# Gate and up of an FFN by Strassen's method: seven block products for eight in 11 of 14 steps

## The reference

```python
def linear(x, w, su, sv):
    return jnp.einsum('bsh,oh->bso', x, w * (su @ sv))
def ffn(x):
    a = linear(x, gate_w, gate_su, gate_sv)     # 1792 x 512
    b = linear(x, up_w, up_su, up_sv)
    return linear(silu(a) * b, down_w, down_su, down_sv)
x = x + 0.5 * ffn(layernorm(x))
x = x + attention(layernorm(x))
x = x + 0.5 * ffn(layernorm(x))
```

## Time and profile before

| what | value |
|---|---|
| median of 3 runs | 1300.13 us (1299.88 to 1300.18) |
| the profiled execution | 1300.31 us, its span in the profile 1299.0 us |
| PE, DVE, ACT, POOL busy | 1270.3, 719.8, 668.6, 403.8 us |
| chain that ended last, PE's share | 95% |

### The profile page before, as it was taken

How to read it: one execution, slowest core, us unless ns; L and a number is a source line. 1 busy time by engine, 2 the same in 40 slices (tenths; PEclk the granted TensorE clock), 3 DMA queues, 4 the chain that set the end, 5 groups by cost and what they waited for, 6 DMA issues and landing times.

```text
span 1299.0 us, 18149 instructions
## 1 busy us (share of the span) xinstructions
PE 1270.3 (98%) x6694; PEld 1084.5 (83%) x6694; DVE 719.8 (55%) x1896; ACT 668.6 (51%) x1623; POOL 403.8 (31%) x331
## 2 busy tenths in 40 slices
PE   5999999999999999999999999999999989999999
PEld 4788888888888888888888888888888878888887
DVE  7443444676566566566566566566566754333333
ACT  3222222247667667667667666666666762222221
POOL 4233222725314315315315315315314321222220
PEclk9999999999999999999999999999999999999999
DMA  7022222101001101001001001001001010111111
GB/s 268 34 101 101 100 86 100 65 2 49 33 1 49 34 1 50 33 1 49 34 1 50 33 1 49 33 1 50 33 1 49 1 49 1 49 49 49 49 49 65
DMA packets 15015, 60.18 MB, mean 46 GB/s; under 512 B 2064, under 2 KB 2736, under 8 KB 12880
## 3 DMA queue, kind: packets, MB, share of 16 engines
q1 hardware_dynamic: 14544, 58.47, 12.4%
q10 hardware_dynamic: 384, 0.56, 0.1%
HBM read 45.91 MB, written 13.11 MB: 45 GB/s over the span
## 4 chain that ended last, share of the span: by engine, by line
PE 95%; DVE 2%; ACT 2%; issue 1%; POOL 0%; DMA 0%; SPq 0%; DVEq 0%; ACTq 0%
PE bank L187 29%; PE bank L188 28%; PE bank L189 28%; PE bank L333 5%; PE bank L312 2%; PE bank L216 1%; PE bank L315 1%; ACT prob L528 0%; ACT prob L537 0%; PE bank L204 0%; POOL w_l_early L879 0%; DMA x_rows<-x 0%; DVE probT_l L798 0%; DVE stats L634 0%; PE bank L199 0%
## 5 line engine op out<-in xcount | busy, mean ns | idle before, releaser
L528 ACT ACTIVATE prob<-prob,neg_top 128x128 f32<-128x128 f32 (+3 forms) x256 | 140.9, 552 | 75.8 <-DVE neg_top L787 75.2
L922 POOL TENSOR_TENSOR rows<-rows,row_root_y 128x640 f32<-128x640 f32 x64 | 80.7, 1261 | 272.2 <-DVE row_root_y L630 272.2
L543 ACT CAST probT_h<-bank 128x512 fp32r<-128x512 f32 x160 | 84.6, 596 | 136.9 <-PE bank L333 136.9
L879 POOL TENSOR_TENSOR w_l_late<-raw_late,w_h_late 128x512 fp32r<-128x512 f32 (+1 forms) x64 | 93.8, 1488 | 178.2 <-ACT w_h_late L425 178.2
L680 DVE TENSOR_TENSOR d<-bank,silu 128x512 f32<-128x512 f32 x56 | 38.7, 691 | 197.3 <-PE bank L189 193.1
L916 POOL TENSOR_TENSOR square<-rows 128x640 f32<-128x640 f32 x64 | 80.3, 1255 | 205.5 <-ACT rows L507 205.5
L537 ACT ACTIVATE prob<-prob,inverse 128x128 f32<-128x128 f32 (+3 forms) x256 | 123.0, 554 | 1.8 <-DVE inverse L792 1.8
L440 ACT CAST d_hi<-d 128x512 fp32r<-128x512 f32 x56 | 34.8, 621 | 168.2 <-DVE d L680 168.2
L187 PE MATMUL bank<-w_h_late,xnT_hi 128*128 128x512 f32 (+1 forms) x352 | 121.2, 344 | 0.0
L189 PE MATMUL bank<-w_h_late,xnT_lo 128*128 128x512 f32 (+1 forms) x352 | 118.6, 337 | 0.0
L188 PE MATMUL bank<-w_l_late,xnT_hi 128*128 128x512 f32 (+1 forms) x352 | 118.3, 336 | 0.0
(11 more groups left out here) (121 smaller groups left out, 3390.5 us busy)
## 6 DMA issues: line engine op xcount, KB each, us to landing
raw_late<-w_qkv SPq DMA_DIRECT2D x8, 1536.0 KB, 6.3
raw_early<-ffn_w SPq DMA_DIRECT2D x21, 512.0 KB, 4.8
scaled<-raw_early SPq DMA_DIRECT2D x21, 512.0 KB, 2.6
raw_late<-scaled SPq DMA_DIRECT2D x21, 512.0 KB, 4.8
raw_late<-w_o SPq DMA_DIRECT2D x8, 1024.0 KB, 4.8
y<-x_rows SPq DMA_DIRECT2D x8, 256.0 KB, 2.0
x_rows<-x SPq DMA_DIRECT2D x6, 256.0 KB, 5.6
x_rows<-x ACTq DMA_DIRECT2D x2, 256.0 KB, 4.4
```

Source lines behind the costliest of these rows:

```text
L528: last = act.activation(p, p, ACT.Exp, bias=neg_top[:, h:h + 1], scale=-1.0, accum_out=total[:, h:h + 1])
L543: act.copy(probT_h[:, j, :, :], banks[r.bank][:, :].rearrange("p (h q) -> p h q", h=G)).then_inc(probT_hi_done, 1)
L879: return pool.tensor_tensor(lo, raw, hi.bitcast(F32), ALU.subtract)
L922: pool.tensor_tensor(row, row, by, ALU.mult).then_inc(rows_normed, 1)
```

## The change

In the steps 1 to 5 of pass 0 and 1 to 6 of pass 1 gate and up are seen as a product of 2 x 2 blocks. The weights' blocks are a11, a12 (chunk 0, features 0 to 255 and 256 to 511) and a21, a22 (chunk 1), the tokens' blocks b11, b21 (batch 0, the two halves of the features) and b12, b22 (batch 1). Eight block products of 12 matmuls become seven, by Strassen's method in Winograd's form: four sums of weight blocks s1 to s4 (`mix_weights`, on GpSimd, each step), four sums of token blocks t1 to t4 (`mix_tokens`, on VectorE, once a pass, from whole tokens that GpSimd and ScalarE put together first), and additions of the products. Products 1, 6, 7 and 4 are added up in the two banks Y (0 and 1) one behind the other; after each of the first three ScalarE copies the partial sum out (`partial_sum`) before the next product may be added. Products 5 and 3 use the two banks Z (2 and 3) in the same way, `down`, the scale products and product 2 the four others. VectorE adds the copies to the banks of products 2, 5 and 3 (`add_up`) and multiplies gate and up from SBUF. All work of `down` and of the scale products stays. `gated(0,0)` of a step comes from products 2 and 1, (c=1, b=1) from 5 and 7, (1,0) from 4, and (0,1) from 3 and 6; the last of them is finished in the next step. The sum blocks get rounded part and rest like all weights.

The core of the diff (PE, then ACT, DVE, POOL):

```diff
+SEVEN = {1: ("a11", "b11", "y"), 2: ("a12", "b21", "x"), 6: ("s2", "t2", "y"), 5: ("s1", "t1", "z"),
+         7: ("s3", "t3", "y"), 4: ("a22", "t4", "y"), 3: ("s4", "b22", "z")}
+Y_BANKS, Z_BANKS = range(0, 2), range(2, 4)
+PLAIN = (0, STEPS - 1), (0,)
+A = ("a11", "a12", "a21", "a22")
...
+            def product(p, s, m):
+                block, tokens, sum_in = SEVEN[m]
+                _, w_h, w_l = place(p, block)
+                pe.wait_ge(ffn_lo, split_nth(p, s, block) + 1)
+                if tokens in MIXES:
+                    at = MIXES.index(tokens)
+                    pe.wait_ge(mix_lo_done, p * len(MIXES) + at + 1)
+                    t_h, t_l = (t[:, at, :, :] for t in mixes[p])
+                else:
+                    k, b = 2 * (int(tokens[1]) - 1), int(tokens[2]) - 1
+                    t_h, t_l = (t[:, k:k + 2, b * S:(b + 1) * S] for t in (xnT_hi, xnT_lo))
+                for half in range(2):
+                    bank = {"x": None, "y": Y_BANKS[half], "z": Z_BANKS[half]}[sum_in]
+                    r, bank = result("product", p, s, m, half, bank=bank)
+                    for k in range(2):
+                        w = slice((2 * k + half) * P, (2 * k + half + 1) * P)
+                        last = matmul3(bank[:, :], (w_h[:, w], w_l[:, w]), (t_h[:, k, :], t_l[:, k, :]),
+                                       k == 0 and m in (1, 2, 5), k == 1, True)
+                    last.then_inc(full[r.bank], 1)
...
+            def ffn_second(p):
+                product(p, 1, 1)
+                product(p, 1, 2)
+                down(p, 0, 1)
+                if p == 0:
+                    scale_weights(1, "down")
+                product(p, 1, 5)
+                product(p, 1, 6)
+                product(p, 1, 7)
+                if p == 0:
+                    scale_weights(2, "gu0")
+                product(p, 1, 4)
+                if p == 0:
+                    scale_weights(2, "gu1")
+                product(p, 1, 3)
             def ffn_step(p, s):
+                product(p, s, 1)
+                down(p, s - 1, 0)
+                if p == 0:
+                    scale_weights(s + 1, "gu0")
+                product(p, s, 2)
+                product(p, s, 6)
+                if p == 0:
+                    scale_weights(s + 1, "gu1")
+                down(p, s - 1, 1)
+                if p == 0:
+                    scale_weights(s, "down")
+                product(p, s, 5)
+                product(p, s, 7)
+                product(p, s, 4)
+                product(p, s, 3)
+            def ffn_last(p):
+                if p == 0:
+                    rotation[0] = range(BANKS)
+                    down(p, STEPS - 2, 0)
+                    gate_up(p, STEPS - 1, 0, 0, (1,))
+                    down(p, STEPS - 2, 1)
+                    scale_weights(STEPS - 1, "down")
+                    gate_up(p, STEPS - 1, 1, 0)
+                    gate_up(p, STEPS - 1, 0, 1, (0,))
+                    down(p, STEPS - 1, 0)
+                else:
+                    down(p, STEPS - 1, 0)
+                    down(p, STEPS - 1, 1)
...
+            def partial_sum(p, s, m, half):
+                r = results["product", p, s, m, half]
+                act.wait_ge(full[r.bank], r.nth)
+                act.copy(more[p][3][:, (1, 6, 7).index(m), half, :], banks[r.bank][:, :]).then_inc(evac[r.bank], 1)
...
+            def mix_hi(p, *ats):
+                for at in ats:
+                    act.wait_ge(mix_done, p * len(MIXES) + MIX_ORDER.index(at) + 1)
+                    act.copy(mixes[p][0][:, at, :, :], mixed_tokens(at)).then_inc(mix_hi_done, 1)
...
+            def ffn_second(p):
+                partial_sum(p, 1, 1, 0)
+                partial_sum(p, 1, 1, 1)
+                split(p, 1, "a22", "s2")
+                silu_of(p, 1, 0, 0)
+                product_hi(p, 1, 0, 0)
+                split(p, 1, "s1")
+                mix_hi(p, 2, 3)
+                split(p, 1, "s3", "s4", "d0", "d1")
+                if p == 0:
+                    stack_factors(2, "gu0")
+                    stack_factors(2, "gu1")
+                partial_sum(p, 1, 6, 0)
+                partial_sum(p, 1, 6, 1)
+                partial_sum(p, 1, 7, 0)
+                silu_of(p, 1, 1, 1)
+                partial_sum(p, 1, 7, 1)
+                silu_of(p, 1, 1, 0)
+                product_hi(p, 1, 1, 1)
+                split(p, 2, "a11")
+                product_hi(p, 1, 1, 0)
+                split(p, 2, "a12")
...
             def ffn_step(p, s):
+                after = s + 1 < STEPS
+                silu_of(p, s - 1, 0, 1)
+                partial_sum(p, s, 1, 0)
+                product_hi(p, s - 1, 0, 1)
+                partial_sum(p, s, 1, 1)
+                split(p, s, "a22", "s2", "s1", "s3", "s4")
+                if p == 0:
+                    stack_factors(s + 1, "gu0")
+                if after:
+                    split(p, s + 1, "a11")
+                silu_of(p, s, 0, 0)
+                if after:
+                    split(p, s + 1, "a12")
+                if p == 0:
+                    stack_factors(s + 1, "gu1")
+                partial_sum(p, s, 6, 0)
+                product_hi(p, s, 0, 0)
+                partial_sum(p, s, 6, 1)
+                if p == 0:
+                    stack_factors(s, "down")
+                split(p, s, "d0", "d1")
+                partial_sum(p, s, 7, 0)
+                silu_of(p, s, 1, 1)
+                partial_sum(p, s, 7, 1)
...
+                    dve.wait_ge(d_done, (p * STEPS + s) * CH * B + at - 1)
+                r = results["product", p, s, m, half]
+                dve.wait_ge(evac[taken.bank], taken.nth)
+                dve.wait_ge(full[r.bank], r.nth)
+                dve.tensor_tensor((d if half else silu)[:, at % 2, :], banks[r.bank][:, :],
+                                  more[p][3][:, (1, 6, 7).index(before), half, :], ALU.add).then_inc(evac[r.bank], 1)
...
+            def ffn_second(p):
+                added_product(p, 1, 0, 0)
+                product_lo(p, 1, 0, 0)
+                down(p, 0, 1)
+                mix_lo(p, 2, 3)
+                if p == 0:
+                    scale_weights(1, "down")
+                added_product(p, 1, 1, 1)
+                if p == 0:
+                    scale_weights(2, "gu0")
+                gated_product(p, 1, 1, 0)
+                product_lo(p, 1, 1, 1)
+                product_lo(p, 1, 1, 0)
+                if p == 0:
+                    scale_weights(2, "gu1")
...
             def ffn_step(p, s):
+                added_product(p, s - 1, 0, 1)
+                product_lo(p, s - 1, 0, 1)
+                down(p, s - 1, 0)
+                if p == 0:
+                    scale_weights(s + 1, "gu0")
+                added_product(p, s, 0, 0)
+                product_lo(p, s, 0, 0)
+                if p == 0:
+                    scale_weights(s + 1, "gu1")
+                down(p, s - 1, 1)
+                if p == 0:
+                    scale_weights(s, "down")
+                added_product(p, s, 1, 1)
+                gated_product(p, s, 1, 0)
+                product_lo(p, s, 1, 1)
+                product_lo(p, s, 1, 0)
...
+            def mix_weights(p, s):
+                if p == 0:
+                    r = results["scale", s, "gu1", 1]
+                    pool.wait_ge(evac[r.bank], r.nth)
+                if s > 1:
+                    pool.wait_ge(ffn_lo, split_nth(p, s - 1, "s4") + 1)
+                a11, a12, a21, a22, s1, s2, s3, s4 = (place(p, block)[0] for block in (*A, "s1", "s2", "s3", "s4"))
+                before = 4 * sevens(p, s) - 4
+                pool.tensor_tensor(s1, a21, a22, ALU.add).then_inc(weights_mixed, 1)
+                pool.wait_ge(weights_mixed, before + 1)
+                pool.tensor_tensor(s2, s1, a11, ALU.subtract).then_inc(weights_mixed, 1)
+                pool.tensor_tensor(s3, a11, a21, ALU.subtract).then_inc(weights_mixed, 1)
+                pool.wait_ge(weights_mixed, before + 2)
+                pool.tensor_tensor(s4, a12, s2, ALU.subtract).then_inc(weights_mixed, 1)
...
+            def whole_tokens(p):
+                r = results["xn", 2 * p, 0, TB - 1]
+                for k in (0, 2):
+                    pool.tensor_tensor(whole[0][:, k:k + 2, :], xnT_hi[:, k:k + 2, 0:S].bitcast(F32), xnT_lo[:, k:k + 2, 0:S].bitcast(F32),
+                                       ALU.add).then_inc(whole_done, 1)
...
             def ffn(p):
...
+                if p == 0:
+                    stack_factors(1, "gu0")
+                whole_tokens(p)
+                if p == 0:
+                    stack_factors(1, "gu1")
+                    stack_factors(1, "down")
+                split(p, 1, "a11", "a12")
+                mix_weights(p, 1)
+                split(p, 1, "a22", "s2", "s1", "s3", "s4", "d0", "d1")
+                if p == 0:
+                    stack_factors(2, "gu0")
+                    stack_factors(2, "gu1")
```

(22 more changed lines are left out.)

452 lines of the change are left out of this document (311 added, 141 removed).

## The result

The changed kernel takes 1305.97 us (median of 5 runs, 1305.43 to 1307.20), the kernel before in the same session 1300.04 (1298.32 to 1300.18): ratio 1.0049, 95% interval 1.0035 to 1.0064. It is slower, by about 6 us or 0.5%; the forecast was 1311, slower. Its profiled execution took 1305.49 us with a span of 1304.2.

What follows compares the result with a forecast made beforehand. PE was taken to bound the kernel, busy 98% of the span. Waits less removed matmuls and the old wait gave pass 0 +12.1, pass 1 -2.9; with refills 1.7, +10.9 on 1300.3: 1311 us, range 1306 to 1315.

Steps and rivals of the forecast that it cites:

- What is removed: Eleven steps lose 12 matmuls each, 132 x 0.227 = 30.0 us; the first step's wait of 0.85 goes, with refill 0.9.
- `down(s-1, 0)` needs block (0,1): Middle steps, both passes: PE waits 0.8 us before this `down` until VectorE's and ScalarE's chain for that block ends.
- the terms 0.8 seven times, 2.9, 1.4, 3.1 and the 3.6 before the second step's `down`: Waits in us, in order: middle steps; pass 1's second step; pass 0's last new step; pass 1's end; pass 0's second step.
- the forecast was -2.9: Pass 1: waits of 13.4 us less 16.3 for removed matmuls, so 2.9 us faster.
- Rival (c): PE's clock falls in long waits, matmuls behind them take 0.43; three waits over 3 us give 5.4: 1316. Chance 0.16.
- the sum of +10.9: Whole kernel: pass 0 +12.1, pass 1 -2.9 and refills 1.7, on the profiled 1300.3 us.
- The exclusion of VectorE and GpSimd: Operations with two SBUF inputs wait for GpSimd's instruction and the reverse; pass 0's first new step waits 4.9, 0.7 without.
- (a): Meetings of VectorE and GpSimd cost nothing at the new places: 1295 us, faster. Chance 0.20.
- (d): Meetings of VectorE and GpSimd cost half: 1303 us, about no change. Chance 0.09.
- (b): PE finds the waits only in part, the chains being too long: down to 1269 us, halfway 1285. Chance 0.09.
- The further 1.3 before product 7: First new step, pass 0: PE waits 1.3 us for `partial_sum(6, 0)`, behind casts of `down`'s weights.
- The waits on `fac`: Pass 0, scale products wait for GpSimd's factor splits: 2.2 (`gu0`) and 0.6 (`gu1`) in middle steps, 4.0 and 0.6 in the second.

Runs made afterwards that it cites:

- Run 3: The changed kernel with `down` of batch 0 also made to wait for the block finished last, (0,1): 1318.4 us.
- run 2: The changed kernel with TensorE running thrown-away matmuls in pass 0's waits on `fac_gu`: 1301.59 us.
- run 4: The changed kernel with VectorE filling the low parts of the four token sums with zeros instead of computing them: 1300.84 us.
- run 1: The changed kernel with pass 0's middle-step factor splits ahead of the five weight casts and rests, their loads one step earlier: 1282.5 us.
- run 9: The changed kernel with the early factor splits and the low parts of the token sums filled with zeros: 1277.81 us.

## Why the prediction was right in sign, and where its terms failed

**What is removed** was right: 132 matmuls at 0.227, and the old wait on `fac_gu`.

**The step that failed** is "`down(s-1, 0)` needs block (0,1)". Blocks are named (c, b): the block that is finished in the next step is chunk 0 of batch 1, and `down(s-1, 0)` takes batch 0. The block is wanted by `down(s-1, 1)`, which comes 24 to 56 matmuls later, behind which its chain is hidden. So the terms 0.8 seven times, 2.9, 1.4, 3.1 and the 3.6 before the second step's `down` do not exist: in the changed kernel no such `down` waits. In pass 0 that changed little: PE reached the scale product earlier and waited there instead, 2.9 for 0.8 + 2.2 and 7.3 for 3.6 + 4.0, for `fac` did not depend on it. In pass 1 no later wait takes them in, and 9.2 of its 13.4 us went: the forecast was -2.9 and the measurement -10.5. Run 3 shows it, by giving the waits back.

**Rival (c), 1316,** was judged at 0.16, and its mechanism came about, as run 2 shows. By the trace it took 7.5 us in pass 0 and 1.6 in pass 1, more than the 5.4 that I gave it, since waits of 2.9 us fall under it too.

**The two errors cancelled, and that was luck.** The dependency made the forecast 9.2 + 1.4 = 10.6 us too slow, the clock 9.1 too fast; and this is why 1311 was near 1306, which lies at the lower edge of the forecast's 1306 to 1315. With both put right the sum of +10.9 becomes +9.4; the sizes of the two first new steps (2.0 and 1.6 below their forecasts) bring it to +5.8, the refills and small waits (2.7 for 1.7) to +6.8, beside the +6.9 of the stages without the start. The sign was luck too: with the dependency alone put right the sum is +0.3, no change. By the balance the slow matmuls, 9.1 us, are more than the whole +6.9, and to them the prediction had given 0.16.

**The exclusion of VectorE and GpSimd** was right in kind; (a) falls, by run 4 and by the rows of `mix_l`, seven of which took 2.2 us or more and one 1.21. Of the 4.2 us that the meetings were to add in the first new step of pass 0, 3.5 came, and in pass 1 2.6 of 4.2, so that (d), half, is too low. (b) falls with the waits on `fac_gu`. In size the first new step of pass 0 had 4.2 against 4.9 forecast, that of pass 1 2.6 against 4.2. The further 1.3 before product 7 did not come. The place was partly another: PE waited first for product 2's bank and for the residual additions, behind `mix_l` in VectorE's list, and only then for s1's rest.

**The waits on `fac`** were right in sum: in the middle steps 0.7 for 0.6 and 2.9 for 0.8 + 2.2, in the second step 7.3 for 3.6 + 4.0.

What stays open: whether the wait that is left in run 1's second step would go with an earlier load; no run parts the load from GpSimd's weight sums, which it follows in SyncE's order. Why equal waits of 2.9 us lower the clock at two places and not at a third, and at other places in another run, is open too; no two profiled executions of one kernel were kept to compare. What bounds the first new step when VectorE and GpSimd have less to do was not tried further than run 9.

## What to carry to other kernels

When work is taken from the engine that bounds, look at what small operations stand behind large ones in the other engines' lists: here two factor splits of 0.7 us stood behind five weight splits of 1.25, and moving them turned +6 us into -17. For each wait that a change adds, check the indices of the dependency in the code as carefully as its price, and put the wait in artificially if in doubt: in the middle steps the price was right to 0.1 us and the dependency wrong. If several orders of the same lists only move a wait, and filling it changes almost nothing either, suspect that the work of the waited-for engines is the bound there, and try less of it (run 9). Compare such orders by stage and not by the whole time alone: here a gain in pass 0 and a loss in pass 1 stood behind an unchanged median.
